# Graph attention and FFN on one core: all five engine lists reordered, PSUM banks assigned anew

## The chip, the core and the metric

The kernel runs on one core of a Trainium2 chip. The core has TensorE (PE, matrix products), VectorE (DVE), ScalarE (ACT), GpSimd (POOL) and SyncE (SP), which here only issues DMAs. Each engine works through a list of its own, in order, and the lists meet only in semaphores. The metric is the device time of one execution in microseconds (us), less is better.

## The reference

Two layers over 64 graphs of 256 nodes with 256 features and 8 heads of 32.

```
layer 0:  q, k = x@Wq + bq, x@Wk + bk;  attn = softmax(q k^T / sqrt(32))
          out  = sum over r of (attn * (adj == r)) @ (x@Wv[r] + bv[r])
          x1   = LN(x + out@Wo + bo);   x2 = LN(x1 + gelu(x1@W1 + b1)@W2 + b2)
layer 1:  q, k, v = x2@Wq, x2@Wk, x2@Wv;   e = leaky(q k^T)
          attn = softmax(where(adj > 0, e, -9e15));   h = LN(attn @ v)
          y    = LN(concat(h, x2) @ Wffn^T) + x2
```

adj holds only 0 and 1 in this data; a general path behind a flag serves other values and does not run.

## The kernel before

A graph passes through four stages, and one turn of the loop works on four graphs at once, one in each stage: `body(g0, g1, g2, g3)`. `turns` (L93) runs turns with some stages missing at both ends, and a hardware loop of full turns between them; 61 of the 67 turns are full. Each engine has its own `body`, a list written out by hand, with a wait in front of each step that needs one. The engines' numbering is offset by one: PE's g2 is the graph that ACT, DVE and POOL call g1 in the same stretch of time. A turn therefore makes one graph of work for every engine, and PE's list of a turn is the same set of products each time.

The steps that the text below speaks of, with their helpers:

- PE, attention of layer 0: `projection("wq")` and `("wk")` and `vee` (values) from the split x; `score_rows(p)` (L1029) for the row maxima; `score_cols(p)` (L1037) for the transposed scores; `both(g)` (weighted values and denominators); `one(g)` (values under the mask adj == 1); `out_projection`.
- PE, FFN: `transposed(B_X1T, x1)`, `up(0..3)`, `down(0..3)`, then `transposed(B_X2T, x2)`.
- PE, layer 1: `projection("lq")`, `("lk")`, `row_products` (lv), `masked_rows(p)` (L960), `turn(p)` (eight transposes of exponentiated scores), `row_values`, `transposed(B_HN, att)` (called the HN transposes below), `transposed(B_N1T, n1)` (the n1 transposes), `half_ffn` twice.
- ACT: `exp_cols(p)` (L529) after each `score_cols`; `exp_rows(p)` (L508); copies out of PSUM (L498); `low(p)` (L502); gelu.
- DVE: `statistics` / `centre` (L680) / `rescale` (L686) are the three pieces of a layer norm, LN_H being that of h in layer 1; `per_head` (L744) in front of it; the split remainders `lo_part` (L659); the comparisons `rel1` (L776) and `off_q` (L811) on the adjacency; `known` (L803), which checks that the adjacency is 0 or 1, and the small minimum `lowest` (L848) behind it.
- POOL: `masked(p)` (L408), two multiplications each, four a graph: the attention weights times rel1, begun when `exp_cols(0)` is done; the remainders `low` (L402); `make_rstd` (L396, L398) for each layer norm.
- SP: `stack(h, dst)` (L309), three DMAs inside SBUF that lay q and k of two heads out for the scores: `stack_a` for layer 0, `stack_r` for layer 1; both read the buffer qk. `load` (L314) brings x, xT, adj and adjT of a graph.

PSUM has eight banks of one 128x512 tile each; `bank(b)` is one, `pair[s]` two neighbours. The table B_... (L200) says which step uses which bank, and a PE step waits until the last reader of its bank is done.

Of the kernel before, what the change touches and what calls it, by code (L numbers as in the profile page):

```python
# [26 lines left out]
H = 8  # L27
# [4 lines left out]
KT = D // P  # L32
# [11 lines left out]
NEG = -9e15  # L44
# [63 lines left out]
def build(nc, x, xT, adj, adjT, w):  # L108
    ctx = ExitStack()
    with ctx:  # L110
# [172 lines left out]
        def _(sp):  # L283
# [42 lines left out]
            def body(g0, g1, g2, g3):  # L326
                if g1 is not None:
                    load(adj_q, adj, g1, "(t p) n -> p t n", ld_adj_r)
                if g2 is not None:
                    stack(0, stack_a, stacked_a)  # L330
                if g3 is not None:
                    load(xt, xT, g3, "(t p) n -> p t n", ld_xt)
                if g2 is not None:
                    stack(2, stack_a, stacked_a)
                    stack(3, stack_a, stacked_a)
                    sp.wait_ge(ashift.sem, ashift.at(g2))
                    for s in range(2):
                        sp.dma_start(stack_a[STK + s:STK + s + 1, 0, :, :].bitcast(F32),
                                     shift_a[32 * s:32 * s + H, :].bitcast(F32)).then_inc(ashifted.sem, 16)
                    if path.general:  # L340
                        load_x_terms(g2)
                if g1 is not None:
# [3 lines left out]
                    stack(2, stack_r, stacked_r)  # L346
                if g3 is not None:
                    if ran(g3, 1):
                        sp.wait_ge(known_done.sem, known_done.at(g3 - 1))
                    load(adj_a, adjT, g3, "(t p) n -> p t n", ld_adj_a)  # L350
                if g1 is not None:
                    stack(3, stack_r, stacked_r)
# [3 lines left out]
                if g3 is not None:  # L356
                    if ran(g3, 1):
                        sp.wait_ge(res_a_done.sem, res_a_done.at(g3 - 1))
                    load(xn, x, g3, "(t p) c -> p t c", ld_xn)
                    sp.wait_ge(qk_split.sem, qk_split.at(g3))  # L360
                    stack(1, stack_a, stacked_a)
# [19 lines left out]
        def _(pool):  # L381
# [48 lines left out]
            def body(g0, g1, g2, g3):  # L430
                if g1 is not None:
                    pool.wait_ge(ln_mv[LN_A].sem, ln_mv[LN_A].at(g1))
# [8 lines left out]
                    low(act_lo[:, 0], act[:, 0], act_hi[:, 0]).then_inc(act_split.sem, 1)  # L441
                if g0 is not None:
# [22 lines left out]
                if g3 is not None:  # L465
                    pool.wait_ge(xt_hi_done.sem, xt_hi_done.at(g3))
                    low(xt_lo[:], xt[:], xt_hi[:]).then_inc(xt_split.sem, 1)
                if g2 is not None:
                    pool.wait_ge(att_hi_done.sem, att_hi_done.at(g2))
                    low(att_lo[:], att[:], att_hi[:]).then_inc(att_split.sem, 1)  # L470
# [20 lines left out]
        def _(act_e):  # L491
# [39 lines left out]
            def body(g0, g1, g2, g3):  # L531
                if g0 is not None:
                    copy(v_r[:], bank(B_LV)).then_inc(rv_done.sem, 1)
                    act_e.wait_ge(sr_mm.sem, sr_mm.at(g0, 2))
                    low(1, B_RR[1]).then_inc(low_done.sem, 1)
                    act_e.wait_ge(sr_mm.sem, sr_mm.at(g0, 3))
                    low(2, B_RR[2]).then_inc(low_done.sem, 1)
                if g2 is not None:
                    act_e.wait_ge(q_mm.sem, q_mm.at(g2, 1))
                    if ran(g2, 2):  # L540
                        act_e.wait_ge(stacked_r[3].sem, stacked_r[3].at(g2 - 2))
                    biased(0, B_Q, bq_c).then_inc(qk_hi_done.sem, 1)
                if g0 is not None:
                    act_e.wait_ge(low_r_done.sem, low_r_done.at(g0, 1))
                    exp_rows(0).then_inc(exp_r_done.sem, 1)
                if g2 is not None:
                    act_e.wait_ge(v_mm.sem, v_mm.at(g2, 1))
                    copy(v_a[:, 0], bank(B_V[0])).then_inc(v_done.sem, 1)
                    act_e.wait_ge(v_mm.sem, v_mm.at(g2))
                    copy(v_a[:, 1], bank(B_V[1])).then_inc(v_done.sem, 1)  # L550
                    act_e.wait_ge(q_mm.sem, q_mm.at(g2))
                    biased(1, B_K, bk_c).then_inc(qk_hi_done.sem, 1)
                if g1 is not None:
                    act_e.wait_ge(x1t_mm.sem, x1t_mm.at(g1))
                    copy(x1t_hi[:], bank(B_X1T)).then_inc(x1t_hi_done.sem, 1)
                if g0 is not None:
                    act_e.wait_ge(turned_mm.sem, turned_mm.at(g0, 1))
                    copy(probs[:, :, 0], pair[B_TN[0]][:]).then_inc(probs_r.sem, 1)
                    act_e.wait_ge(sr_mm.sem, sr_mm.at(g0))
                    low(3, B_RR[3]).then_inc(low_done.sem, 1)  # L560
                if g1 is not None:
# [5 lines left out]
                    gelu(2, B_UP[2]).then_inc(act_done.sem, 1)  # L567
                    act_e.wait_ge(act_split.sem, act_split.at(g1, 1))
                    act_e.wait_ge(up_mm.sem, up_mm.at(g1))
                    gelu(3, B_UP[3]).then_inc(act_done.sem, 1)  # L570
                if g0 is not None:
                    act_e.wait_ge(low_r_done.sem, low_r_done.at(g0, 2))
                    exp_rows(1).then_inc(exp_r_done.sem, 1)
# [4 lines left out]
                    act_e.wait_ge(turned_mm.sem, turned_mm.at(g0, 2))  # L578
                    copy(probs[:, :, 1], pair[B_TN[1]][:]).then_inc(probs_r.sem, 1)
# [27 lines left out]
                if g1 is not None:  # L607
                    act_e.wait_ge(sr_mm.sem, sr_mm.at(g1, 1))
                    low(0, B_RR[0]).then_inc(low_done.sem, 1)

# [16 lines left out]
        def _(dve):  # L627
# [121 lines left out]
            def body(g0, g1, g2, g3):  # L749
                if g2 is not None:  # L750
                    dve.wait_ge(qk_hi_done.sem, qk_hi_done.at(g2))
                    biased_low(1, B_K, bk_c).then_inc(qk_split.sem, 1)
                if g1 is not None:
                    dve.wait_ge(x1t_hi_done.sem, x1t_hi_done.at(g1))
                    lo_part(x1t_lo, B_X1T, x1t_hi).then_inc(x1t_split.sem, 1)
                if g0 is not None:
                    dve.wait_ge(low_done.sem, low_done.at(g0, 3))
                    leaky(2, B_RR[2]).then_inc(leaky_done.sem, 1)
                    dve.wait_ge(leaky_done.sem, leaky_done.at(g0, 2))
                    lowest_row(1).then_inc(low_r_done.sem, 1)  # L760
# [521 lines left out]
```

## Time and profile before

| | us |
|---|---|
| median of 3 runs | 3328.57 |
| lowest and highest | 3326.73, 3330.99 |
| profiled execution, its time | 3329.45 |
| profiled execution, its span | 3327.6 |
| PE busy / DVE busy / ACT busy / POOL busy | 3141.7 / 2795.0 / 2098.1 / 1474.6 |
| mean granted TensorE clock | 0.991 of full |

The profile page gives busy times per engine, the span in 40 slices, the DMA queues, the chain that ended last and the costliest groups of instructions. The trace behind it answers by engine, line, tile and stretch. A PE row of two matmuls such as `1526.04 0.40 ... x2` starts the next such row 0.235 us later: matmuls overlap, and their ends are modelled.

### The profile page before, as it was taken

How to read it: one execution, taken by the hardware profiler on the slowest of the kernel's cores; microseconds unless marked ns; L12 is line 12 of the kernel's file. 1: busy time of each engine (PE TensorE's matmuls, PEld its weight loads, DVE VectorE, ACT ScalarE, POOL GpSimd, SP SyncE). 2: the span in 40 equal slices, each digit the busy share in tenths (PEclk: the TensorE clock that was granted, in tenths of full speed). 3: DMA queues.
4: the chain of work that ended last, by engine and by line, in shares of the span. 5: the costliest groups of instructions: out<-in, count | busy, mean ns of one | idle time of the engine just before them, and what ended most of it. 6: DMA issues, size and time to landing. Idle time of an engine off the chain costs nothing.

```text
span 3327.6 us, 77390 instructions
## 1 busy us (share of the span) xinstructions
PE 3141.7 (94%) x28930; PEld 2713.8 (82%) x28930; DVE 2795.0 (84%) x4892; ACT 2098.1 (63%) x4300; POOL 1474.6 (44%) x1549
## 2 busy tenths in 40 slices
PE   3899999999999999999999999999999999999996
PEld 2788888888888888888888888888888888888885
DVE  3688888888888888888888888888888888888885
ACT  2466666666666666666666666666666666666664
POOL 1345345344444444444444444444444444444441
PEclk8999999999999999999999999999999999999998
DMA  3333333333433433423433433433433433433331
GB/s 105 81 89 82 101 81 86 102 79 85 105 76 86 107 76 86 107 76 86 107 76 86 107 76 86 107 76 86 107 76 86 107 76 86 106 77 86 104 74 33
DMA packets 217643, 292.63 MB, mean 88 GB/s; under 512 B 31492, under 2 KB 119048, under 8 KB 217608
## 3 DMA queue, kind: packets, MB, share of 16 engines
q1 hardware_dynamic: 217608, 292.16, 34.2%
q8 instruction: 22, 0.36, 0.0%
q14 instruction: 13, 0.11, 0.0%
HBM read 72.89 MB, written 16.78 MB: 27 GB/s over the span
## 4 chain that ended last, share of the span: by engine, by line
PE 62%; SPq 10%; DVE 7%; POOL 7%; DMA 6%; ACT 4%; issue 4%; POOLq 0%; DVEq 0%; ACTq 0%
PE pair L920 32%; PE pair L950 11%; SPq L309 8%; DMA stack_a<-qk 5%; PE pair L974 5%; POOL probs L408 4%; PE pair L1033 3%; PE pair L965 3%; DVE n L686 3%; PE pair L966 3%; ACT probs L529 2%; POOL rstd L398 2%; PE pair L925 2%; DVE qk L738 2%; ACT qk L516 2%
## 5 line engine op out<-in xcount | busy, mean ns | idle before, releaser
L402 POOL TENSOR_TENSOR act_r_lo<-act,act_r_hi 128x512 fp32r<-128x512 f32 x256 | 345.7, 1356 | 654.0 <-DVE act_r_hi L765 523.0
L502 ACT ACTIVATE leaky_s<-pair 128x1024 f32<-128x1024 f32 x256 | 260.5, 1029 | 436.6 <-PE pair L966 436.6
L508 ACT ACTIVATE leaky_s<-leaky_s,low_r 128x256 f32<-128x256 f32 x1024 | 506.6, 496 | 10.9 <-DVE low_r L728 4.1
L732 DVE TENSOR_REDUCE mx_a<-pair 128x4 f32<-128x1024 f32 x256 | 306.4, 1217 | 114.0 <-PE pair L1033 113.9
L408 POOL TENSOR_TENSOR probs<-probs,rel 128x512 f32<-128x512 f32 x256 | 309.6, 1229 | 164.2 <-ACT probs L529 164.2
L396 POOL TENSOR_TENSOR rstd<-mv,eps 128x2 f32<-128x2 f32 x256 | 72.6, 284 | 660.0 <-DVE mv L675 660.0
L529 ACT ACTIVATE probs<-pair 128x1024 f32<-128x1024 f32 x256 | 263.1, 1029 | 127.8 <-PE pair L1042 125.4
L498 ACT ACTIVATE probs<-pair 128x1024 f32<-128x1024 f32 x256 | 260.5, 1019 | 86.2 <-PE pair L974 81.9
L724 DVE TENSOR_TENSOR leaky_s<-pair,leaky_s 128x1024 f32<-128x1024 f32 x256 | 306.7, 1219 | 5.2 <-ACT leaky_s L502 5.2
L728 DVE TENSOR_REDUCE low_r<-leaky_s 128x4 f32<-128x1024 f32 x256 | 304.0, 1208 | 0.0
L408 POOL TENSOR_TENSOR leaky_s<-probs,rel 128x512 f32<-128x512 f32 x256 | 300.7, 1204 | 0.0
L974 PE MATMUL pair<-ident,leaky_s 128*128 128x128 f32 x2048 | 267.8, 274 | 10.0 <-ACT leaky_s L508 9.8
L965 PE MATMUL pair<-stack_r 96*128 96x256 f32 x1024 | 271.6, 360 | 4.9 <-DMA stack_r<-qk 2.3
L966 PE MATMUL pair<-off_q,identb 128*128 128x256 bf16 x1024 | 259.4, 285 | 0.0
L523 ACT ACTIVATE act<-pair,bias_col 128x256 f32<-128x256 f32 x512 | 209.7, 473 | 73.6 <-PE pair L920 72.8
L974 PEld LDWEIGHTS pair<-ident,leaky_s 128*128 128x128 f32 x2048 | 231.3, 141 | 13.1 <-ACT leaky_s L508 11.1
L920 PE MATMUL pair<-xt_r_hi,w_hi 128*128 128x256 f32 x1024 | 209.5, 286 | 29.0 <-DVE xt_r_lo L659 29.0
L965 PEld LDWEIGHTS pair<-stack_r 96*128 96x128 f32 x1024 | 205.1, 200 | 32.0 <-issue 28.8
L853 DVE RECIPROCAL att<-pair 128x512 f32<-128x512 f32 x64 | 214.9, 3358 | 14.6 <-PE pair L950 12.6
L398 POOL TENSOR_TENSOR rstd<-rstd,power 128x2 f32<-128x2 f32 x256 | 216.3, 845 | 20.1
L950 PE MATMUL pair<-probs,v_a 128*32 128x256 f32 x3072 | 205.7, 386 | 13.3 <-ACT probs L529 13.3
L402 POOL TENSOR_TENSOR att_r_lo<-att,att_r_hi 128x512 fp32r<-128x512 f32 x64 | 82.6, 1290 | 305.2 <-DVE att_r_hi L864 305.2
(180 smaller groups left out, 9112.3 us busy)
## 6 DMA issues: line engine op xcount, KB each, us to landing
stack_a<-qk SPq DMA_DIRECT2D x768, 128.0 KB, 2.9
stack_r<-qk SPq DMA_DIRECT2D x768, 128.0 KB, 2.4
xt<-in_xT SPq DMA_DIRECT2D x64, 256.0 KB, 3.2
adj_a<-in_adjT SPq DMA_DIRECT2D x64, 256.0 KB, 3.1
xn<-in_x SPq DMA_DIRECT2D x64, 256.0 KB, 3.0
adj_q<-in_adj SPq DMA_DIRECT2D x64, 256.0 KB, 3.0
out<-n SPq DMA_DIRECT2D x64, 256.0 KB, 2.2
probs<-in_w SPq DMA_DIRECT2D x4, 512.0 KB, 5.1
```

The source lines that it names most:

```text
L402: return nc.gpsimd.tensor_tensor(dst, src, hi, ALU.subtract)
L408: last = nc.gpsimd.tensor_tensor(masked_p[g][:, h], probs[:, g, h], rel1[:], ALU.mult)
L508: last = nc.scalar.activation(leaky_s[:, p % SLOTS, k, t], leaky_s[:, p % SLOTS, k, t], ACT.Exp, bias=low_r[:, p, k, t:t + 1], accum_out=d ...
L529: return nc.scalar.activation(probs[:, g, 2 * q:2 * q + 2], pair[b][:], ACT.Exp, scale=SCALE)
L724: return nc.vector.tensor_tensor(leaky_s[:, p % SLOTS], pair[b][:], leaky_s[:, p % SLOTS], ALU.max)
L728: return nc.vector.tensor_reduce(low_r[:, p], leaky_s[:, p % SLOTS], AX.X, ALU.max, negate=True)
L732: return nc.vector.tensor_reduce(mx_a[:, :, p * NG:(p + 1) * NG].rearrange("p t h -> p h t"), pair[b][:], AX.X, ALU.max)
L920: last = mm(dst, lhs(i, t), rhs(j, t), start=start and n == 0, stop=stop and n == len(steps) - 1, skip_group_check=skip)
L950: last = mm(bank(b)[h * DH:(h + 1) * DH, g, :], v(t, g * GH + h), pr(h, t), start=first and t == 0, stop=stop and t == NT - 1, skip_group_ ...
L965: mm(dst, stack_r[:, 0, slot(h), t * P:(t + 1) * P], stack_r[:, 1, slot(h), :], start=True, stop=False)
L966: last = mm(dst, identb[:], off_q[:, t, :], start=False, stop=True)
L974: last = nc.tensor.transpose(pair[b][:, k, c, t * P:(t + 1) * P], leaky_s[:, p % SLOTS, k, t, c * P:(c + 1) * P], ident[:])
```

## The change

No instruction is added or removed on any engine; every list is put in another order and the banks are given out anew. What the text below speaks of:

- PE: `score_cols(1)` comes directly after `score_cols(0)`, and the HN transposes after both; `masked_rows(1)` and `(2)` of a graph move to the next turn, around the q projection; `turn(0)` moves ahead of the k projection, `turn(1)` ahead of the up products; `down(3)` moves behind `turn(3)`; `one(0)` moves from ahead of the second half of the FFN to behind `masked_rows(0)`.
- DVE: in the stretch of LN_H, `off_q` comes in ahead of `centre`, and `known` in the place of the x cast between `centre` and `rescale`; the cast and the reciprocal of the row sums move ahead to `shift`; `rel1` moves behind the statistics of the FFN's norm; `lowest` leaves the place ahead of the long reciprocal.
- POOL: the remainder of the next x ahead of the masks instead of behind them; that of the attention output at the head of the next turn.
- SP: all four `stack_a` copies in one row behind the split of k; in the kernel before, copy 1, a load, copy 0, a load, copies 2 and 3.
- ACT: `exp_rows(1)` before the first turned copy, the turned copy 1 between gelu 2 and gelu 3, the bias on k last.

```diff
-        B_AO, B_ADEN, B_Q, B_K, B_WO, B_X1T, B_RV, B_HN = 2, 4, 3, 7, 4, 6, 3, 4
-        B_DN, B_N1T, B_FFN, B_AMT, B_X2T, B_LQ, B_LK, B_LV = 3, 3, 0, 7, 5, 3, 6, 1
+        B_AO, B_ADEN, B_Q, B_K, B_WO, B_X1T, B_RV, B_HN = 2, 6, 7, 6, 1, 4, 4, 2
+        B_DN, B_N1T, B_FFN, B_AMT, B_X2T, B_LQ, B_LK, B_LV = 1, 1, 3, 4, 1, 4, 7, 7
         B_X = 0
-        B_V, B_UP = (5, 4), (7, 1, 3, 2)
-        B_RR, B_TN, B_AR, B_AC = (2, 3, 0, 2), (1, 0, 2, 1), (0, 3, 2, 3), (3, 1, 3, 3)
+        B_V, B_UP = (5, 7), (4, 6, 1, 5)
+        B_RR, B_TN, B_AR, B_AC = (0, 2, 1, 0), (0, 1, 1, 3), (3, 1, 2, 3), (2, 3, 2, 0)
...
# SP, behind the stack_r copies
+                if g3 is not None:
+                    sp.wait_ge(qk_split.sem, qk_split.at(g3))
+                    stack(0, stack_a, stacked_a)
+                    stack(1, stack_a, stacked_a)
+                    stack(2, stack_a, stacked_a)
+                    stack(3, stack_a, stacked_a)
                     load(adj_a, adjT, g3, "(t p) n -> p t n", ld_adj_a)
...
# POOL, behind the four act remainders, ahead of the masks
+                if g3 is not None:
+                    pool.wait_ge(xt_hi_done.sem, xt_hi_done.at(g3))
+                    low(xt_lo[:], xt[:], xt_hi[:]).then_inc(xt_split.sem, 1)
...
# DVE, the stretch of LN_H
                     lo_part(x2t_lo, B_X2T, x2t_hi).then_inc(x2t_split.sem, 1)
+                    dve.wait_ge(ld_adj_r.sem, ld_adj_r.at(g1))
+                    nc.vector.tensor_scalar(off_q[:], adj_q[:], 0, NEG, ALU.is_le, ALU.mult).then_inc(off_done.sem, 1)
                 if g0 is not None:
                     dve.wait_ge(ln_mv[LN_H].sem, ln_mv[LN_H].at(g0))
                     centre(LN_H, n1, LG1, n1)
-                if g3 is not None:
-                    dve.wait_ge(ld_xt.sem, ld_xt.at(g3))
-                    nc.vector.tensor_copy(xt_hi[:], xt[:]).then_inc(xt_hi_done.sem, 1)
+                if g2 is not None and not path.general:
+                    dve.wait_ge(rel1_done.sem, rel1_done.at(g2))
+                    nc.vector.scalar_tensor_tensor(adj_a[:], adj_a[:], 0, rel1[:], ALU.is_equal, ALU.add,
+                                                   accum_out=known[:]).then_inc(known_done.sem, 1)
                 if g0 is not None:
                     dve.wait_ge(ln_mid[LN_H].sem, ln_mid[LN_H].at(g0))
                     dve.wait_ge(ln_rstd[LN_H].sem, ln_rstd[LN_H].at(g0))
...
# DVE, end of the turn: x1's remainder, then k's, in this order
+                    dve.wait_ge(x1t_hi_done.sem, x1t_hi_done.at(g2))
+                    lo_part(x1t_lo, B_X1T, x1t_hi).then_inc(x1t_split.sem, 1)
+                if g3 is not None:
+                    dve.wait_ge(qk_hi_done.sem, qk_hi_done.at(g3))
+                    biased_low(1, B_K, bk_c).then_inc(qk_split.sem, 1)
...
# PE, after the row values
                     pe.wait_ge(ashifted.sem, ashifted.at(g3))
+                    if ran(g3, 2):
+                        pe.wait_ge(att_r_done.sem, att_r_done.at(g3 - 2))
                     score_cols(0, B_AC[0]).then_inc(sta_mm.sem, 1)
+                    score_cols(1, B_AC[1]).then_inc(sta_mm.sem, 1)
                 if g1 is not None:
                     pe.wait_ge(att_r_done.sem, att_r_done.at(g1))
                     transposed(B_HN, att).then_inc(hn_mm.sem, 1)
-                if g3 is not None:
-                    score_cols(1, B_AC[1]).then_inc(sta_mm.sem, 1)
...
# PE, the n1 transposes: no longer behind the q split of layer 1
                 if g1 is not None:
-                    if ran(g1, -1):
-                        pe.wait_ge(rqk_split.sem, rqk_split.at(g1 + 1, 1))
+                    if ran(g1, -2):
+                        pe.wait_ge(probs_a.sem, probs_a.at(g1 + 2))
                     pe.wait_ge(ln_done[LN_H].sem, ln_done[LN_H].at(g1))
                     transposed(B_N1T, n1).then_inc(n1t_mm.sem, 1)
...
# PE, ahead of the up products
+                    pe.wait_ge(leaky_done.sem, leaky_done.at(g1, 3))
+                    turn(1, B_TN[1]).then_inc(turned_mm.sem, 1)
                 if g2 is not None:
                     pe.wait_ge(x1t_split.sem, x1t_split.at(g2))
                     up(0, B_UP[0]).then_inc(up_mm.sem, 1)
```

## Rows read from the trace of the kernel before

**Rows 1.** Page, part 5: group, count | busy us, mean ns | idle before, releaser.

```profile
L974 PE MATMUL pair<-ident,leaky_s 128*128 128x128 f32 x2048 | 267.8, 274 | 10.0 <-ACT leaky_s L508 9.8
```

**Rows 2.** Busy time by stretch: PE, PEld, DVE, ACT, POOL, then clock, DMA share, GB/s.

```profile
600.00:3100.00 2500.00, 2432.02 (x22574) 2103.95 (x22574) 2168.84 (x3796) 1627.74 (x3346) 1151.45 (x1200) 1.00 0.35 89
```

**Rows 3.** Waits of PE, 600 to 3100 us: total us, times, longest.

```profile
PE pair L1033 <- DMA stack_a<-qk: 21.8, 68, 0.7
PE pair L920 <- DVE xt_r_lo L659: 21.3, 49, 0.4
PE pair L938 <- DVE qk L840: 10.7, 50, 0.2
PE pair L950 <- ACT probs L529: 9.8, 50, 0.2
```

**Rows 4.** PE's timeline, one turn: start, us, line, operation, [idle before].

```profile
1520.56 0.74 PE L1042 MATMUL pair<-stack_a 98*128 98x256 f32 x4
1521.35 0.66 PE L938 MATMUL pair<-ident,att 128*128 128x128 f32 x4
...
1523.60 1.07 PE L950 MATMUL pair<-probs,v_a 128*32 128x256 f32 x16 [0.20 <-ACT probs L529]
...
1526.04 0.40 PE L920 MATMUL pair<-x2t_hi,lq_hi 128*128 128x256 f32 x2
...
1529.25 0.65 PE L938 MATMUL pair<-ident,n 128*128 128x128 f32 x4 [0.22 <-DVE qk L840]
...
1548.10 0.60 PE L938 MATMUL pair<-ident,x 128*128 128x128 f32 x4
...
1550.11 0.50 PE L920 MATMUL pair<-xt_r_hi,w_hi 128*128 128x256 f32 x2 [0.44 <-DVE xt_r_lo L659]
...
1556.15 1.21 PE L1033 MATMUL pair<-stack_a 96*128 96x256 f32 x8 [0.33 <-DMA stack_a<-qk]
...
1559.11 0.73 PE L1033 MATMUL pair<-stack_a 96*128 96x256 f32 x4 [0.37 <-DMA stack_a<-qk]
```

**Rows 5.** DVE's timeline, the same turn, the stretch of LN_H.

```profile
1522.16 0.69 DVE L744 TENSOR_TENSOR n<-pair,rden_r 128x512 f32<-128x512 f32 x1 [0.72 <-PE pair L938]
...
1524.07 0.69 DVE L659 TENSOR_TENSOR x2t_lo<-pair,x2t_hi 128x512 fp32r<-128x512 f32 x1
1524.67 0.88 DVE L680 SCALAR_TENSOR_TENSOR n<-n,mv,norm 128x256 f32<-128x256 f32 x2
1525.47 0.42 DVE L833 CAST xt_r_hi<-xt 128x512 fp32r<-128x512 f32 x1
1526.03 1.17 DVE L686 SCALAR_TENSOR_TENSOR n<-n,rstd,norm 128x256 f32<-128x256 f32 x1
1527.13 1.39 DVE L686 SCALAR_TENSOR_TENSOR n<-n,rstd,norm 128x256 f32<-128x256 f32 x1
```

**Rows 6.** POOL's timeline beside it: the mask multiplications.

```profile
1522.44 2.29 POOL L408 TENSOR_TENSOR probs<-probs,rel 128x512 f32<-128x512 f32 x2 [2.15 <-ACT probs L529]
...
1525.67 1.25 POOL L408 TENSOR_TENSOR probs<-probs,rel 128x512 f32<-128x512 f32 x1
1526.88 1.36 POOL L408 TENSOR_TENSOR probs<-probs,rel 128x512 f32<-128x512 f32 x1
```

**Rows 7.** DVE's timeline: known and lowest, and x1's remainder.

```profile
1518.46 0.66 DVE L803 SCALAR_TENSOR_TENSOR adj_a<-adj_a,rel 128x512 int32<-128x512 int32 x1
...
1531.18 0.62 DVE L848 TENSOR_TENSOR lowest<-lowest,known 128x1 f32<-128x1 f32 x1
...
1549.37 0.69 DVE L659 TENSOR_TENSOR xt_r_lo<-pair,xt_r_hi 128x512 fp32r<-128x512 f32 x1 [0.19 <-ACT xt_r_hi L498]
```

**Rows 8.** SP's timeline: six stack_a issues in a row.

```profile
1504.76 3.80 SPq L309 DMA_DIRECT2D stack_a<-qk  x6
```

**Rows 9.** The profile page, part 6: issues, KB, us from issue to landing.

```profile
stack_a<-qk SPq DMA_DIRECT2D x768, 128.0 KB, 2.9
stack_r<-qk SPq DMA_DIRECT2D x768, 128.0 KB, 2.4
```

More of the change, by code:

```diff
@@ L326, in body @@
             def body(g0, g1, g2, g3):
-                if g1 is not None:
-                    load(adj_q, adj, g1, "(t p) n -> p t n", ld_adj_r)
                 if g2 is not None:
-                    stack(0, stack_a, stacked_a)
+                    load(xn, x, g2, "(t p) c -> p t c", ld_xn)
                 if g3 is not None:
@@ L555, in body @@
                     copy(x1t_hi[:], bank(B_X1T)).then_inc(x1t_hi_done.sem, 1)
+                if g2 is not None:
+                    act_e.wait_ge(v_mm.sem, v_mm.at(g2))
+                    copy(v_a[:, 1], bank(B_V[1])).then_inc(v_done.sem, 1)
                 if g0 is not None:
-                    act_e.wait_ge(turned_mm.sem, turned_mm.at(g0, 1))
-                    copy(probs[:, :, 0], pair[B_TN[0]][:]).then_inc(probs_r.sem, 1)
                     act_e.wait_ge(sr_mm.sem, sr_mm.at(g0))
@@ L567, in body @@
                     gelu(2, B_UP[2]).then_inc(act_done.sem, 1)
+                if g0 is not None:
+                    act_e.wait_ge(turned_mm.sem, turned_mm.at(g0, 2))
+                    copy(probs[:, :, 1], pair[B_TN[1]][:]).then_inc(probs_r.sem, 1)
+                if g1 is not None:
                     act_e.wait_ge(act_split.sem, act_split.at(g1, 1))
@@ L795, in body @@
                     nc.vector.tensor_tensor(res[:], bank(B_DN), x1[:], ALU.add).then_inc(res_m_done.sem, 1)
-                if g2 is not None:
-                    dve.wait_ge(amt_mm.sem, amt_mm.at(g2))
-                    shift(bank(B_AMT)[0:H, 0, :], shift_a, g2, ashift_hi, ashift)
-                if g1 is not None:
                     dve.wait_ge(res_m_done.sem, res_m_done.at(g1))
                     statistics(LN_M, res, g1)
-                if g2 is not None and not path.general:
-                    nc.vector.scalar_tensor_tensor(adj_a[:], adj_a[:], 0, rel1[:], ALU.is_equal, ALU.add,
-                                                   accum_out=known[:]).then_inc(known_done.sem, 1)
+                if g2 is not None:
+                    dve.wait_ge(ld_adj_a.sem, ld_adj_a.at(g2))
+                    nc.vector.tensor_scalar(rel1[:], adj_a[:], 1, None, ALU.is_equal).then_inc(rel1_done.sem, 1)
                 if g1 is not None:
@@ L845, in body @@
                     lo_part(n1t_lo, B_N1T, n1t_hi).then_inc(n1t_split.sem, 1)
-                if g2 is not None and not path.general:
-                    dve.wait_ge(known_done.sem, known_done.at(g2))
-                    nc.vector.tensor_tensor(lowest[:], lowest[:], known[:], ALU.min).then_inc(lowest_done.sem, 1)
                 if g2 is not None:
@@ L858, in body @@
                     centre(LN_O, bank(B_FFN), LG2, result)
+                if g1 is not None:
+                    dve.wait_ge(low_done.sem, low_done.at(g1, 1))
+                    leaky(0, B_RR[0]).then_inc(leaky_done.sem, 1)
                 if g2 is not None:
@@ L1144, in body @@
                     down(1)
+                if g3 is not None:
+                    pe.wait_ge(mx_a_done.sem, mx_a_done.at(g3, 1))
+                    pe.wait_ge(stacked_a[3].sem, stacked_a[3].at(g3))
+                    score_rows(3, B_AR[3]).then_inc(sa_mm.sem, 1)
+                if g2 is not None:
                     pe.wait_ge(act_split.sem, act_split.at(g2, 3))
```

248 lines of the change are left out of this document (115 added, 133 removed).

## Prediction

> **What bounds the kernel now.** The page comes first: PE is busy 94% of the span, DVE 84%. Then the busy time by stretch: from 600 to 3100 us PE is busy 2432.0 of 2500 us at full clock [rows 2]. In PE's timeline the same step comes round every 50.0 us, one turn, so PE is the bound, short of some waits. The waits of PE name four, 63.6 us in 50 turns, 1.27 us a turn [rows 3]. That understates them. A matmul's modelled end lies 0.16 us past the start of its successor (0.40 long, 0.235 apart), so a wait costs its idle bracket plus 0.16. By the timeline [rows 4] a turn loses: ahead of up(0), for x1's remainder, 0.44+0.16 = 0.60; ahead of score_rows(0), for the stack_a copies, 0.49; ahead of score_rows(2), again for them, 0.53; ahead of both(0), for exp_cols, 0.36; ahead of the n1 transposes, for the q remainder of layer 1 that holds their bank, 0.38; and ahead of the HN transposes 0.22 without a bracket (score_cols(0) at 1520.56 takes 0.57 where nothing waits, the transposes start 0.79 later). Sum 2.58 us of 50.0: about 47.4 us are products, and the change leaves these alone. Only the waits can move, from -2.6 us a turn to any loss.
>
> **Part by part.** Letters: S is the start of score_cols(0), P that of x1's transposes.
>
> *The wait ahead of up(0), 0.60.* x1's transposes start at P, the remainder on DVE at P+1.27 (1548.10, 1549.37) and ends at P+1.96 [rows 4, 7]. New, turn(1) stands between masked_rows(3) and up(0). A turn is 267.8/256 = 1.05 us busy, less the overlap 0.89 [rows 1]. PE arrives at up(0) 0.89 later than the P+1.4 of before, at P+2.3, after the remainder. Gain 0.60. Turn(1) itself waits for leaky(2), which DVE does while PE is at vee(1) and the transposes; I take nothing for it, at most 0.3.
>
> *The stack_a copies, 0.49 and 0.53.* New, DVE makes the remainder of k behind that of x1: P+1.27, then 0.60 on (the distance of such rows at 1524.07 and 1524.67 [rows 5]) and two instructions of 0.88 together: P+2.75. SP then issues twelve copies without a load between, 3.80/6 = 0.63 apart [rows 8]. Those of score_rows(2) are complete with the ninth: P+2.8+8x0.63 = P+7.8, plus 2.4 us to landing as for stack_r, which also goes out in one row, or 2.9 as for stack_a now [rows 9]: P+10.2 to P+10.8. PE wants them at: 1559.11-1548.10 = 11.0, less the three waits of before, 1.62, plus turn(1), 0.89, so P+10.3. Wait 0 to 0.5; I take 0.3, the middle, as the copies are like stack_r's but more of them compete. Score_rows(0) needs the third copy, P+4.1+2.9 = P+7.0, and is wanted at about P+7.7: no wait. Gain 0.49+0.23 = 0.72.
>
> *HN transposes and exp_cols.* With score_cols(1) pulled ahead, the transposes start at S+1.13 after the copy of the row values is done: gain 0.22. The wait for exp_cols(1) ahead of both(0) stays, 0.36. From S to the lq projection it was 1526.04-1520.56 = 5.48; without the 0.22 it is 5.26 [rows 4]. And HN is now 0.34 later after S than before (0.79).
>
> *The norm LN_H, where I expect the loss.* Before: DVE's per_head starts 0.81 after HN, x2t_lo 1.91 after that, centre (two instructions), the x cast, and rescale, whose instructions take 1.17 and 1.39 us where such an instruction alone takes under 0.5 (centre, 0.88 for two) [rows 4, 5]. Beside them POOL multiplies the masks: 1525.67 to 1526.92, then a row starting 1526.88 that lasts 1.36 instead of 1.15 [rows 6]. The first rescale ends 0.28 after the first multiplication, the second 0.28 after the next (1528.24): the two engines take turns, one DVE instruction per multiplication, 1.31 us a pair. The little lowest, one element a partition, takes 0.62 there [rows 7]. So each DVE instruction of this kind that is caught behind the masks costs about 1.3 us.
>
> New list: per_head at S+1.13+0.81 = S+1.94, x2t_lo at S+3.85, off_q at S+4.45, centre at S+4.79 and S+5.19, known at S+5.6, rescale. POOL's third multiplication (the first that matters) keeps its distance: 1525.67-1522.44 = 3.23 behind the first, which starts 1.88 behind S: S+5.11 [rows 4, 6]. It comes between the two centre instructions. Known, which comes ahead of rescale in place of a cast, is then caught, and rescale twice, against two catches before. If the second centre instruction gets in first: multiplication to S+6.65, known (0.66 alone, 0.5 of it held [rows 7]) to S+7.2, multiplication to S+8.3, rescale to S+8.55, multiplication to S+9.7, rescale to S+9.95. If it is caught too, one more pair: S+10.8. PE comes to the n1 transposes at S+5.26+2.84 = S+8.10 (2.84: from 1526.04 to 1529.25 less 0.38). Wait 1.9 or 2.8 us against 0.38. The two starts lie 0.08 us apart, nearer than I can tell, so I take 2.4: loss 2.0. Neither known nor centre is seen beside a mask in this trace. The bounds: no new catch at all, then LN_H is done by S+8.95 at the latest with both rescales caught (wait 0.9, loss 0.5), or by S+7.2 with none (no wait, gain 0.4); at the other end both caught and off_q too, loss 3.4.
>
> The Trainium skill, "SBUF — State Buffer", section "Who interferes with whom", has a rule for this: a VectorE instruction with two SBUF inputs, or in a two-port mode, and a GpSimd instruction that reads SBUF hold the shared port pair exclusively, each for its whole length. By that rule known (adj_a and rel1) and centre (n and norm) are caught like rescale, and the loss is the 2.0; by the rows alone, were only rescale caught, it would be 0.5, and the sum a gain. This case's 1.17 and 1.39 us against 0.48 agree with the rule for rescale only.
>
> *Behind it.* The q and k remainders of layer 1 stand behind rescale on DVE, the twelve stack_r copies on SP behind them, masked_rows(0) on PE. All shift with the n1 transposes: the third copy lands 1.3+1.3+2.4 = 5.0 after rescale, PE arrives there 5.1 after (n1 transposes 0.4; both(1) 1.87, from 1523.60 to 1526.04 less 0.57; the FFN half and lv 1.42 each, like lq). No further wait, at most 0.2. The later output projection meets the attention remainder, which POOL now makes first: att_split follows one(1) by some 3 us and four steps lie between; nothing taken.
>
> *Edits at nothing.* The x cast and remainder ahead of the masks: POOL is busy 46% [rows 2] and idle there. rel1 and the reciprocals: DVE has 6.6 us free a turn. The turned copy between two gelus lies on ACT, a third free. If the covers go, each costs its own 0.4 to 1.3 us once a turn; PE would show it as a wait at the x2 transposes. Fill and drain, 3329.45-64x50.0 = 129 us in all, are reordered too; I take 0, within 5 either way.
>
> **Sum.** A turn: -0.60 - 0.72 - 0.22 + 2.0 = +0.46 us. 61 full turns: +28 us on the profiled execution's 3329.45, which lies 0.9 above the median: 3357 for the median.
>
> **Rivals.**
> 1. *Known and centre slip in ahead of the masks, or aren't held by them* (faster). For it: 0.08 us decide the order, and nobody has seen known held here. Against it: lowest, a still smaller instruction, is. The wait at n1 is then 0 to 0.9, loss at most 0.5: -1.54+0.5 = -1.0 a turn, -63 us: 3266; with no wait at all 3211. It decides if LN_H is done before S+8.10+0.38+1.54 = S+10.0, where gains and loss cancel; the less, the faster.
> 2. *Both centre and known caught, and stack copies at 2.9 us* (clearly slower). -0.60-0.22-0.49+2.4+0.2 = +1.3 a turn: 3408. For it: the waiting engine took its turn at 1526.88. Against: the cheaper landing of a run of copies.
> 3. *It cancels.* Centre in first and copies landing at 2.4: -0.60-1.02-0.22+1.55 = -0.3; with small waits at turn(1) and masked_rows(0) 0.0: within 7 us of 3328.6. PE stays the bound and the change only moves waits.
>
> **Chances.** Forecast 42%, rival 1 26%, rival 2 18%, rival 3 14%. 0.2% is 6.7 us, about what a measurement of this kernel can tell from no change. Faster by more 0.26, within 0.14, slower 0.60. The range 3262 to 3405 reaches to the middle of rival 1 and the edge of rival 2; the forecast's own is 3338 to 3390.
>
> **What would show it.** The waits of PE: no row for xt_r_lo ahead of up, one for the n1 transposes (PE L938 on DVE n L686) of some 2 us a turn. On DVE, known at 1.2 us or more instead of 0.66, and a rescale of n still at 1.2 to 1.4. Stack_a: one wait a turn, under 0.6. The prediction is wrong if PE waits under 1 us for n, or if known keeps 0.66: then look for rival 1; and if PE shows a wait at turn(1), masked_rows(0) or out_projection that I set at nothing.

## The result, and the profile after

The changed kernel took 3254.16 us (median of 4 runs, 3245.96 to 3258.36) against 3328.11 us for the kernel before (3326.73 to 3330.99), a ratio of 0.977 with a 95% interval of 0.975 to 0.979. The forecast was slower, 3357 us, range 3262 to 3405. It was wrong in sign, and the time lies below the range; of the cases named, rival 1 came closest (3266 with small losses, 3211 with none).

The page and the window and wait views of after, with the columns of the rows of before [rows 1 to 3, 9]:

```profile
PE 3119.1 (96%) x28930; PEld 2711.1 (83%) x28930; DVE 2710.2 (83%) x4892; ACT 2063.7 (63%) x4300; POOL 1473.1 (45%) x1549
L976 PE MATMUL pair<-ident,leaky_s 128*128 128x128 f32 x2048 | 269.6, 275 | 6.7 <-ACT leaky_s L502 5.8
...
stack_a<-qk SPq DMA_DIRECT2D x768, 128.0 KB, 2.4
stack_r<-qk SPq DMA_DIRECT2D x768, 128.0 KB, 2.4
```

```profile
600.00:3100.00 2500.00, 2469.69 (x23132) 2153.17 (x23130) 2147.82 (x3891) 1638.33 (x3422) 1177.29 (x1230) 1.00 0.39 91
```

```profile
PE pair L940 <- DVE n L686: 21.1, 51, 0.5
PE pair L952 <- ACT probs L523: 9.1, 51, 0.2
```

PE is busy 2469.7 of 2500 us, where it was 2432.0 [rows 2], at the full clock in both. The remainder of x1 and the stack_a copies are gone from its waits [rows 3]. The 10.7 us for the q remainder have become 21.1 us for n, that is for the end of LN_H, in 51 turns: 0.41 us each, where about 2.2 was forecast (2.4 with the 0.16 by which a bracket understates a wait). A copy of stack_a now lands in 2.4 us instead of 2.9 [rows 9]. A turn, measured from one start of score_cols(0) (S) to the next and averaged from 600 to 3000 us, fell from 50.08 to 48.88 us. 61 turns times 1.20 are 73 us, and the medians differ by 74: nothing of note happened in fill and drain.

PE's timeline of after, one turn (start, us, line, operation, [idle before]); it answers to [rows 4]:

```profile
1513.51 1.04 PE L976 MATMUL pair<-ident,leaky_s 128*128 128x128 f32 x8
1514.30 0.48 PE L922 MATMUL pair<-xt_r_hi,w_hi 128*128 128x256 f32 x2
...
1521.91 1.36 PE L1035 MATMUL pair<-stack_a 96*128 96x256 f32 x8
...
1533.49 1.12 PE L1044 MATMUL pair<-stack_a 98*128 98x256 f32 x8
1534.45 0.60 PE L940 MATMUL pair<-ident,att 128*128 128x128 f32 x4
...
1536.16 1.07 PE L952 MATMUL pair<-probs,v_a 128*32 128x256 f32 x16 [0.18 <-ACT probs L523]
...
1538.60 0.40 PE L922 MATMUL pair<-x2t_hi,lq_hi 128*128 128x256 f32 x2
...
1542.01 0.66 PE L940 MATMUL pair<-ident,n 128*128 128x128 f32 x4 [0.41 <-DVE n L686]
```

The up products at 1514.30 and the two score_rows of stack_a at 1521.91 start without a wait. The heads' transposes start at S + 0.96, lq at S + 5.11 (before: 5.48), and n1's transposes at S + 8.52 (before: 8.69).

DVE and POOL of after in the stretch of LN_H, S = 1533.49; they answer to [rows 5, 6]:

```profile
1535.20 0.69 DVE L744 TENSOR_TENSOR n<-pair,rden_r 128x512 f32<-128x512 f32 x1 [0.84 <-PE pair L940]
...
1536.94 0.66 DVE L659 TENSOR_TENSOR x2t_lo<-pair,x2t_hi 128x512 fp32r<-128x512 f32 x1
1537.52 0.41 DVE L805 TENSOR_SCALAR off_q<-adj_q 128x512 bf16<-128x512 int32 x1
1537.85 0.87 DVE L680 SCALAR_TENSOR_TENSOR n<-n,mv,norm 128x256 f32<-128x256 f32 x2
1538.64 0.68 DVE L811 SCALAR_TENSOR_TENSOR adj_a<-adj_a,rel 128x512 int32<-128x512 int32 x1
...
1539.25 2.70 DVE L686 SCALAR_TENSOR_TENSOR n<-n,rstd,norm 128x256 f32<-128x256 f32 x2
```

```profile
1537.60 0.39 POOL L390 TENSOR_TENSOR rstd<-mv,eps 128x2 f32<-128x2 f32 x1
1538.06 0.81 POOL L392 TENSOR_TENSOR rstd<-rstd,power 128x2 f32<-128x2 f32 x1
1538.84 2.83 POOL L402 TENSOR_TENSOR probs<-probs,rel 128x512 f32<-128x512 f32 x2
```

Known (DVE L811) takes 0.68 us, against 0.66 in before, where POOL did not hold it [rows 7]. The third mask multiplication is the first of the two on the last line. It starts at 1538.84, 0.20 us behind known, instead of ahead of it. The two rescales take 2.70 us together, two catches as before.

### The profile page after: what moved, and what is told of

It reads as the page before. It is cut to its first block, busy times and chain, and to the rows that moved or that the text cites. A ratio compares the mean times of both kernels' runs of the same rounds, so it can differ in the third digit from the quotient of the medians.

```text
span 3252.1 us, 77634 instructions
## 1 busy us (share of the span) xinstructions
PE 3119.1 (96%) x28930; PEld 2711.1 (83%) x28930; DVE 2710.2 (83%) x4892; ACT 2063.7 (63%) x4300; POOL 1473.1 (45%) x1549
## 4 chain that ended last, share of the span: by engine, by line
PE 81%; DVE 14%; issue 2%; SPq 1%; DMA 1%; ACT 1%; POOL 0%; DVEq 0%; ACTq 0%; POOLq 0%
PE pair L922 44%; PE pair L952 11%; PE pair L976 7%; DVE n L686 5%; PE pair L1035 4%; PE pair L967 4%; PE pair L968 4%; PE pair L940 3%; PE pair L1044 2%; PE pair L927 2%; DVE n L680 2%; DVE n L744 1%; DVE x2t_lo L659 1%; DVE stats L671 1%; SPq L309 1%
## 5 line engine op out<-in xcount | busy, mean ns | idle before, releaser
L396 POOL TENSOR_TENSOR act_r_lo<-act,act_r_hi 128x512 fp32r<-128x512 f32 x256 | 334.8, 1315 | 748.7 <-DVE act_r_hi L886 550.3
L402 POOL TENSOR_TENSOR probs<-probs,rel 128x512 f32<-128x512 f32 x256 | 327.2, 1300 | 124.7 <-ACT probs L523 124.7
L492 ACT ACTIVATE v_r<-pair 128x512 f32<-128x512 f32 x64 | 38.2, 597 | 269.8 <-PE pair L922 269.8
L922 PE MATMUL pair<-w_hi,act_r_hi 128*128 128x256 f32 x1024 | 208.8, 286 | 0.0
```

The costliest lines, as they stand in the source:

```text
L396: return nc.gpsimd.tensor_tensor(dst, src, hi, ALU.subtract)
L402: last = nc.gpsimd.tensor_tensor(masked_p[g][:, h], probs[:, g, h], rel1[:], ALU.mult)
L492: return nc.scalar.activation(dst, src, ACT.Copy)
L922: last = mm(dst, lhs(i, t), rhs(j, t), start=start and n == 0, stop=stop and n == len(steps) - 1, skip_group_check=skip)
```

## The experiments

Turns are means from 600 to 3000 us; S is the start of score_cols(0), and the starts of n1's transposes are medians over the same turns. Each run's interval for the ratio to before, 95%, stands in the table; before was run anew beside each group of runs, with medians of 3327.84 to 3330.45 us. A delay is given as the shift of off_q's start; the expectations call the three 0.36, about 0.56 and 0.72 us.

| kernel | us | ratio to before | turn, us | n1's transposes |
|---|---|---|---|---|
| before | 3328.11 | 1 | 50.08 | S+8.68 |
| after | 3254.16 | 0.975 to 0.979 | 48.88 | S+8.52 |
| a1: delay 0.33 | 3273.21 | 0.981 to 0.985 | 49.17 | S+8.84 |
| a10: delay 0.53 | 3441.82 | 1.032 to 1.035 | 51.88 | S+10.89 |
| a2: delay 0.66 | 3495.98 | 1.049 to 1.053 | 52.56 | S+11.02 |
| a3: known late | 3231.92 | 0.969 to 0.972 | 48.55 | S+8.17 |
| a9: off_q early | 3278.48 | 0.983 to 0.986 | 49.23 | S+8.83 |
| a8: both | 3237.69 | 0.971 to 0.973 | 48.56 | S+8.23 |
| a11: a8, masked_rows together | 3254.71 | 0.976 to 0.979 | 48.88 | S+8.24 |
| a4: HN between the scores | 3252.61 | 0.976 to 0.979 | 48.85 | S+8.51 |
| a5: turn(1) back | 3282.25 | 0.984 to 0.988 | 49.45 | not moved |
| a6: loads between the copies | 3405.25 | 1.021 to 1.025 | 51.19 | not moved |
| b1: before, known in LN_H | 3441.76 | 1.032 to 1.036 | 51.96 | S+10.25 |
| b2: before, copies in a row | 3270.98 | 0.981 to 0.984 | 49.13 | S+8.68 |

### Is the forecast's mechanism real? Delays of LN_H (a1, a10, a2)

Into DVE's list of the kernel after, ahead of off_q, one or two statistics of n1 that nobody uses (a10: the second one over 128 columns of a constant). In this and the later cuts, waits, guards and loops around the lines are left out:

```
                 lo_part(x2t_lo, B_X2T, x2t_hi).then_inc(x2t_split.sem, 1)
+                nc.vector.bn_stats(spare[:, 0], n1[:, 0])           # a1, a10, a2
+                nc.vector.bn_stats(spare[:, 1], n1[:, 1])           # a2
+                nc.vector.bn_stats(spare[:, 1], norm[:, 0, 0:128])  # a10
                 nc.vector.tensor_scalar(off_q[:], adj_q[:], 0, NEG, ALU.is_le, ALU.mult)
```

> The changed kernel with one more statistics instruction (0.36 us, one SBUF input, its result unused) on VectorE between x2t_lo and off_q. Theory of turns: known is issued 0.2 us ahead of the third mask multiplication in the changed kernel; with 0.36 more it comes behind it, is caught, and each later pair of instructions takes turns: LN_H ends about 1.2 us later, the wait of PE ahead of the n1 transposes grows from 0.57 to about 1.8 a turn, known lasts over 1.0 us, and the time is 3254 + 61x1.2 = 3327. Rival, queue length alone: LN_H ends 0.36 later, the time is 3254 + 22 = 3276, known stays at 0.68.

> As the one before with two such instructions, 0.72 us. Theory of turns: the second centre instruction is caught too, LN_H ends about 2.4 us later than in the changed kernel: 3254 + 61x2.4 = 3400. Rival, queue length alone: 3254 + 61x0.72 = 3298.

> The kernel after with 0.36 + about 0.2 us of statistics into an unused buffer between x2's low part and off_q, half-way between the two delays already run (0.36 us: 3273; 0.72 us: 3496). Theory (a cliff: as soon as the third mask product starts ahead of the second centring or of known, VectorE's instruction waits for its end): known or centring is stretched by about 1 us, n1's transposes start 1.3 us or more later than in the kernel after, and the total is at least 3254 + 61 x 1.5 = 3345 us, more where PE's clock falls. Rival (queue length alone, 61 x 0.57): 3289 us.

One delay cost 19 us, what its length asks for (n1's transposes 0.32 us later), so the expectation of a caught known missed. A further 0.2 us cost 169 us more. Between the two lies the step that the forecast had assumed. DVE and POOL of a10, S = 1463.4:

```profile
1467.93 0.41 DVE L811 TENSOR_SCALAR off_q<-adj_q 128x512 bf16<-128x512 int32 x1
1468.26 1.79 DVE L681 SCALAR_TENSOR_TENSOR n<-n,mv,norm 128x256 f32<-128x256 f32 x2
1469.97 1.66 DVE L817 SCALAR_TENSOR_TENSOR adj_a<-adj_a,rel 128x512 int32<-128x512 int32 x1
...
1471.56 2.65 DVE L687 SCALAR_TENSOR_TENSOR n<-n,rstd,norm 128x256 f32<-128x256 f32 x2
```

```profile
1467.76 0.69 POOL L393 TENSOR_TENSOR rstd<-rstd,power 128x2 f32<-128x2 f32 x1
1468.41 2.67 POOL L403 TENSOR_TENSOR probs<-probs,rel 128x512 f32<-128x512 f32 x2
```

The mask multiplication starts at 1468.41, while the first centre instruction runs, and has its turn before the second. So the second centre instruction takes 1.40 us (medians over the turns; 1.79 for the two here against 0.87 in after), known 1.66 instead of 0.68, and n1's transposes start at S + 10.89. In a1 the mask multiplication also starts ahead of known, by 0.19 us, and yet known keeps 0.69: the row that begins first is here not the one that goes first. DVE and POOL of a1:

```profile
1507.56 0.88 DVE L681 SCALAR_TENSOR_TENSOR n<-n,mv,norm 128x256 f32<-128x256 f32 x2
1508.35 0.69 DVE L816 SCALAR_TENSOR_TENSOR adj_a<-adj_a,rel 128x512 int32<-128x512 int32 x1
```

```profile
1507.25 0.94 POOL L393 TENSOR_TENSOR rstd<-rstd,power 128x2 f32<-128x2 f32 x1
1508.16 3.21 POOL L403 TENSOR_TENSOR probs<-probs,rel 128x512 f32<-128x512 f32 x2
```

There POOL is the one that is held. The first of its two multiplications lasts 1.91 us (median) instead of 1.17, about to the end of known and one undisturbed length on. A reading that fits, but is not shown: once DVE had what both need, its next instruction followed without a gap that POOL could use. In a10, with DVE's starts 0.2 us later, POOL got in. What exactly decides who has the next turn is not settled by these runs. That 0.2 us decide it is shown.

### Known alone (a3 and b1)

In after known is moved behind the low part of n1's transposes (a3). In before it is moved the other way, between the x cast and the rescales (b1):

```
a3:              centre(LN_H, n1, LG1, n1)
-                nc.vector.scalar_tensor_tensor(adj_a[:], adj_a[:], 0, rel1[:], ...accum_out=known[:])
                 rescale(LN_H, n1, row(LB1))
                 ...
                 lo_part(n1t_lo, B_N1T, n1t_hi).then_inc(n1t_split.sem, 1)
+                nc.vector.scalar_tensor_tensor(adj_a[:], adj_a[:], 0, rel1[:], ...accum_out=known[:])
b1:              nc.vector.tensor_copy(xt_hi[:], xt[:])
+                nc.vector.scalar_tensor_tensor(adj_a[:], adj_a[:], 0, rel1[:], ...accum_out=known[:])
```

> The changed kernel with known moved out of the norm LN_H, behind n1t_lo. Theory: rescale follows centre at once, LN_H ends 0.6 us or more earlier and PE's wait ahead of the n1 transposes (0.57 a turn) goes: 3254 - 61x0.57 = 3219. Rival: known, now caught beside the masks (1.2 us), pushes the long reciprocal and what hangs on it, and PE waits ahead of out_projection instead: within 7 us of 3254.

> The kernel before with known moved into LN_H, between the x cast and rescale, as the change has it, and nothing else. Theory of turns: the cast starts 0.2 us ahead of the third mask multiplication there, so known comes behind it and is caught: known lasts 1.1 us or more, LN_H ends 1.3 to 1.6 us later, the n1 transposes wait that much more: 3328 + 61x1.3 = 3407. Rival, queue length alone: known's own 0.74 at most, 3328 + 45 = 3373, or nothing if the gap ahead of rescale hides it.

a3 is the fastest kernel of the study: 3231.92 us, 22 us below after. Its only wait of PE from 600 to 3100 us with a bracket is this one:

```profile
PE pair L952 <- ACT probs L523: 9.3, 52, 0.2
```

The expectation of 3219 had the whole wait of 0.57 us go. Only 0.35 went (S + 8.52 to S + 8.17). The rescales now start at S + 5.49, 0.10 us behind the end of POOL's power (the reciprocal root of LN_H, S + 5.39), and LN_H ends at S + 8.12; PE still waits for it, too briefly for a bracket.

b1 shows the forecast's number where the order is the forecast's: DVE and POOL of b1.

```profile
1525.84 1.66 DVE L832 SCALAR_TENSOR_TENSOR adj_a<-adj_a,rel 128x512 int32<-128x512 int32 x1
...
1527.43 2.68 DVE L686 SCALAR_TENSOR_TENSOR n<-n,rstd,norm 128x256 f32<-128x256 f32 x2
```

```profile
1525.70 2.83 POOL L408 TENSOR_TENSOR probs<-probs,rel 128x512 f32<-128x512 f32 x2
```

The multiplication starts 0.14 us ahead of known, known takes 1.66 us, both rescales are caught behind it, and n1's transposes start 1.57 us later than in before. So "a DVE instruction with two operands in SBUF, caught behind the masks, costs a turn" holds for known (1.66) and for centre (1.40 in a10), not for rescale alone. This is the exclusive lock that the Trainium skill gives in "SBUF — State Buffer", section "Who interferes with whom", and the traces agree in both directions: 1.66 us for known here, 1.91 us for the multiplication in a1.

### What else stands ahead of the rescales (a4, a9, a8)

```
a4 (PE):         score_cols(0, B_AC[0]).then_inc(sta_mm.sem, 1)
+                transposed(B_HN, att).then_inc(hn_mm.sem, 1)
                 score_cols(1, B_AC[1]).then_inc(sta_mm.sem, 1)
-                transposed(B_HN, att).then_inc(hn_mm.sem, 1)
a9 (DVE):        rescale(LN_M, x2, row(E2))
+                nc.vector.tensor_scalar(off_q[:], adj_q[:], 0, NEG, ALU.is_le, ALU.mult)
                 ...
                 lo_part(x2t_lo, B_X2T, x2t_hi).then_inc(x2t_split.sem, 1)
-                nc.vector.tensor_scalar(off_q[:], adj_q[:], 0, NEG, ALU.is_le, ALU.mult)
a8: the edits of a3 and a9 together
```

> The changed kernel with the HN transposes back between score_cols(0) and score_cols(1), on PE alone. Theory: per_head and all of LN_H on VectorE come 0.45 us earlier, the wait at the n1 transposes goes, exp_cols(1) is not later since ScalarE is still at exp_cols(0): 3254 - 61x0.5 = 3224. Rival: exp_cols(1) comes later by the 0.4 us and both(0) waits that much more: 3254 within 10 us.

> The kernel after with off_q alone moved ahead of per_head; known stays between centring and rescaling. Theory (a long VectorE instruction is stretched if it starts while GpSimd holds what they share, and off_q's 0.42 us are the only gain): known starts 0.4 us earlier, ahead of the third mask product, and is not stretched; the two rescalings are stretched as in the kernel after; n1's transposes start at S + 8.3 and the total is 3240 to 3254 us. Rival (the queue's length alone counts, and the earlier rescalings fall outside the third mask product too): 3219 us.

> The kernel after with two VectorE instructions taken out of the stretch between the transposed heads and the norm's rescale: the sum over the mask products (known, 0.68 us) moved behind the low part of n1's transposes, and the adjacency mask off_q moved ahead of per_head. Theory (the norm's end sets the start of n1's transposes, and both instructions lie in its way): the kernel with known alone moved took 3232 us and the wait ahead of n1's transposes still held about 0.2 to 0.4 us a turn through off_q and the centring; off_q gone moves centring 0.4 us earlier, n1's transposes start at S + 7.8, and the total is 3232 - 61 x 0.38 = 3209 us. Rival (ScalarE's and GpSimd's reciprocal root, which ends at S + 5.1, holds the rescaling, so that an earlier centring gains nothing): 3225 to 3232 us. Rival (off_q ahead of per_head delays per_head itself): 3240 us.

None gained on the kernel it started from (after for a4 and a9, a3 for a8). In a4 per_head starts 0.48 us earlier, but off_q then falls beside the second mask multiplication, lasts 0.68 instead of 0.41, and centre starts at S + 4.36 as in after. The time is the rival's, the reason is not: both(0) starts where it did in after, at S + 2.68 against 2.67. In a9 centre and known are 0.33 us earlier, and the cost is 24 us. DVE and POOL of a9:

```profile
1498.81 0.87 DVE L680 SCALAR_TENSOR_TENSOR n<-n,mv,norm 128x256 f32<-128x256 f32 x2
1499.60 0.69 DVE L811 SCALAR_TENSOR_TENSOR adj_a<-adj_a,rel 128x512 int32<-128x512 int32 x1
...
1500.93 2.62 DVE L686 SCALAR_TENSOR_TENSOR n<-n,rstd,norm 128x256 f32<-128x256 f32 x2 [0.64 <-POOL rstd L392]
```

```profile
1499.42 1.41 POOL L392 TENSOR_TENSOR rstd<-rstd,power 128x2 f32<-128x2 f32 x1
```

Here the small power on POOL, two numbers a partition, is the one that waits: it lasts 1.41 us instead of 0.81 and ends 0.55 us behind known (S + 6.05 and S + 5.50, medians), and the rescales wait for it (0.64 us). Of the two expectations neither had this. In a8 known is away, and the power ends at S + 5.45, 0.55 us behind the second centre instruction; in a3 it ends at S + 5.39. So the rescales start at S + 5.55, and in a3 at S + 5.49, though centre is 0.33 us earlier in a8: the rival with the power as the limit had the right mechanism (3238, 6 us over the end of its 3225 to 3232). The third guess, 3240, is nearer as a number, but per_head is not delayed: it starts at S + 1.72 as in after. a8's turn equals a3's (48.56 and 48.55); the 6 us between their medians lie outside the stretch from 600 to 3000 us, and what makes them was not followed.

### The gains one by one (b2, a5, a6)

```
b2 (before, SP):   stack 0, stack 2, stack 3 in a row, then the loads of adj_q and xt
                   (were ahead of and behind stack 0; stack 1 is issued earlier in both)
a5 (after, PE):    turn(1) behind the up products instead of ahead of them
a6 (after, SP):    stack 0, load adj_q, stack 1, load adj_a, stack 2, stack 3 (was: adj_q, stacks 0 to 3, adj_a)
```

> The kernel before with the stack_a copies of a graph issued in one row, the two loads behind them. Theory: the waits ahead of score_rows(0) and (2), 0.37 and 0.35 a turn on average, go: 3328 - 61x0.7 = 3285. Rival: what counts is when the remainder of k is done, not the loads between: half of it or less stays, 3306 or more.

> The changed kernel with turn(1) behind the up products instead of ahead. Theory: PE waits 0.6 us a turn for x1's remainder ahead of up(0), as before the change: 3254 + 37 = 3291. Rival: the stack_a copies then have the slack that turn(1) gives, and a wait is only moved: under 3270.

> The changed kernel with the loads of adj_q and adj_a put between the stack_a copies (behind copy 0 and behind copy 1), as before the change. Theory: the issues of copy 2 end 1.1 us later and land 0.5 later: score_rows(2) waits 0.9 to 1.3 us: 3254 + 61x1.1 = 3321. Rival: landing has slack of 1 us here: under 3270.

b2 is 57 us faster than before with nothing else changed, 0.95 us a turn: PE's waits for stack_a are gone and the copy lands in 2.4 us. The two steps ahead of score products that waited are shorter by 0.35 and 0.37 us, the score products behind them by 0.10 and 0.09. a5 gives back 28 us, 0.57 a turn, and the wait for x1's remainder comes back as it was [rows 3]:

```profile
PE pair L922 <- DVE xt_r_lo L659: 21.7, 50, 0.4
```

a6 puts two loads between the copies: it costs 151 us, far over the 67 expected. The page gives 2.9 us for a landing again, and PE waited for stack_a 86.1 us in 52 places between 600 and 3000 us, 2.5 us at most. With the 0.16 that a bracket leaves out that is 2.0 us a turn, 123 us in 61 turns; the rest is the clock (last section). Why the wait is nearly twice the 1.1 us expected was not followed.

### One change of kind fewer on PE (a11)

```
-                masked_rows(1, B_RR[1]).then_inc(sr_mm.sem, 1)
                 ... (wq)
+                masked_rows(1, B_RR[1]).then_inc(sr_mm.sem, 1)
                 masked_rows(2, B_RR[2]).then_inc(sr_mm.sem, 1)
```

> The kernel with both instructions moved (a8_both_moved), and PE's masked_rows(1) put directly ahead of masked_rows(2), so that the order is wq, masked_rows(1), masked_rows(2) in place of masked_rows(1), wq, masked_rows(2). Theory (each change from one kind of product to another costs PE about 0.085 us, by the step lengths): one change fewer, 61 x 0.085 = 5 us below a8_both_moved. Rival (changes of kind cost nothing by themselves, only the order against other engines does): equal within 2 us, or above it where the later scores hold ScalarE or VectorE.

A miss: 17 us slower than a8. The two masked_rows together take 1.874 us instead of 1.903, so the boundary gave 0.03, not 0.085, and wq and wo beside it are 0.02 longer each. But the value projection ahead of the first turn takes 1.83 instead of 1.63 us, and the turn behind it 0.85 instead of 0.79: the second pair's scores come one projection later. That what waits for them is later too would explain it, but which engine holds PE there was not followed.

## Why the prediction was wrong, step by step

**The wait ahead of up(0): right.** Forecast gain 0.60; from the start of masked_rows(3) to that of the next step it was 1.657 us and is 1.058. a5 puts turn(1) back and loses 0.57. Turn(1) waits for nothing.

**The stack_a copies: mechanism right, the sum met by luck.** Forecast gain 0.72, of it 0.49 and 0.23. The waits that went are 0.37 and 0.35 on average (my one turn had shown 0.49 and 0.53), so the whole loss was 0.72, and all of it went: of the two landings the cheap one, 2.4 us, came true. By b2 the repair alone is worth 0.95 a turn, because the products behind a wait were longer too. I had kept 0.3 for a wait that doesn't exist, and taken 1.02 instead of 0.72 for the loss; the two errors cancel.

**HN transposes and exp_cols: right.** From S to lq went from 5.48 to 5.11, 0.37 where 0.22 was forecast. In a4, where the HN transposes follow score_cols(0) as in before, they start at S + 0.48 and not S + 0.79: that step takes 0.48 us and not 0.57, so the wait had been 0.31. The wait for exp_cols stays at 0.35.

**The norm LN_H: this step failed.** Forecast: loss 2.0 a turn, n1's transposes at S + 10.0 to 10.9. Measured: S + 8.52, a wait of 0.57 (0.41 bracket and 0.16) where 0.38 stood, a loss of 0.19. PE's arrival there, forecast for S + 8.10, is S + 7.95 (lq at S + 5.11, and 2.84 us for lq and lk without a wait); that part was near. What failed is the order of centre, known and the third mask multiplication. By the steps of the forecast, medians over the turns of after:

| start behind S | forecast | after |
|---|---|---|
| HN transposes | 1.13 | 0.96 |
| per_head | 1.94 | 1.72 |
| x2t_lo | 3.85 | 3.45 |
| off_q | 4.45 | 4.03 |
| centre, both | 4.79, 5.19 | 4.36, 4.76 |
| known | 5.6 | 5.15 |
| third mask multiplication | 5.11 | 5.36 |

Two errors add up to 0.7 us. DVE's list runs 0.4 us earlier than I had it: 0.17 from the start of HN, 0.05 in per_head, and 0.17 because I carried over 1.91 us from per_head to x2t_lo, where the statistics between them take 1.74 and the rest had been a wait. And the third multiplication is 0.25 later, since it does not keep its distance from the first: between them stands POOL's reciprocal root, whose first instruction lasts 0.39 instead of 0.20 beside off_q, which makes 0.18 of it. (In a1 a statistics instruction stands in off_q's place at the same start, and POOL's instruction lasts 0.19.) So known starts 0.2 us ahead of the multiplication and not 0.5 behind it. I had put the margin at 0.08 us "nearer than I can tell", and nevertheless split it only between one catch and two; that both instructions could slip in ahead needed a shift of no more than 0.5 us, and had 26%.

The mechanism itself stands. Delay the stretch by 0.53 us and the very sequence of the second branch appears: a10's transposes start at S + 10.89, where the forecast gave S + 10.8 for both caught, and it takes 3442 us. The order and the catches are as forecast; that the two ends lie so near is partly luck, since one more pair of 1.31 us on the forecast's S + 9.95 would be S + 11.3. Known beside a mask is 1.66 us in a10 and b1, as the sequence needs. It was the phase that was wrong, far more than the price.

**Behind it, and the edits at nothing: one term missing.** No wait came at turn(1), masked_rows(0) or the output projection. But the steps in which PE waits for nothing became longer by 0.30 in sum. The larger parts, which make 0.25 of it, are the down products 5.74 to 6.02 us, wo and wk 0.08 each, score_rows 0.05, less 0.07 in wf and 0.08 each in the turns and masked_rows. Part of it is seen at the starts: the first product of a step of another kind is 0.48 long and followed after 0.32 instead of 0.235 us. a11 shows that this is no fixed price of a boundary (0.03, not 0.085). Where the rest comes from stays open: no run takes the new bank table or ACT's new order alone.

**The sum.** -0.60 for x1, -0.72 for the copies, -0.37 from S to lq, +0.19 at n1, +0.30 in the products: -1.20 us a turn, as measured. Forecast +0.46; of the difference of 1.66 the norm makes 1.8, S to lq 0.15 and the products -0.30.

The conclusion "known keeps 0.66: then look for rival 1" was the right test. Rival 1's own number, 3266, was made with a loss of 0.5 at n1; with the 0.19 measured it would be 3246, 8 us too low, since the products' +0.30 outweighs the extra 0.15 from S to lq.

## What to carry to other kernels

A wait of one turn read from a timeline is a sample: take averages, and ask of each distance that is carried over whether a wait is in it. Where a forecast hangs on which of two instructions on different engines starts first and they lie within half a microsecond, it has two answers, not a middle: give both prices and an even chance, or make the margin large. The same holds for tuning: the fast order of this kernel lies 0.3 to 0.5 us from one that costs 190 us more, and moving the one DVE instruction out of the critical stretch (a3) gains 22 us. It also takes known out of the danger; centre stays in it, and no run delays a3. Put the copies that a product waits for in one row and the loads behind them: in the kernel before that alone gave 57 us (b2), where the whole change gave 74.

## What the runs showed of the hardware

**PE's clock fell after the long waits.** In before, after, a1 and a3 PE's granted clock is 1.00 from 600 to 3000 us. In a10 the turns come in two lengths, 51.3 us (27 of 45) and 52.8 us (18 of 45); the granted clock is 1.00 over each of the short ones and 0.97 over each of the long ones. Two turns of a10 by stretch (columns as in [rows 2]); the first line of each group is the wait for n, and the first group is a short turn, the second a long one:

```profile
1473.00:1474.30 1.30, 0.03 (x1) 0.04 (x1) 1.30 (x2) 0.00 (x0) 1.30 (x2) 1.00 0.00 0
1474.30:1475.30 1.00, 1.00 (x12) 0.67 (x16) 1.00 (x2) 0.34 (x1) 1.00 (x2) 1.00 0.00 0
1475.30:1476.30 1.00, 1.00 (x24) 0.65 (x20) 0.80 (x2) 0.26 (x1) 1.00 (x1) 1.00 0.00 0
...
1524.30:1525.60 1.30, 0.00 (x0) 0.00 (x0) 1.30 (x2) 0.00 (x0) 1.30 (x2) 1.00 0.00 0
1525.60:1526.60 1.00, 0.98 (x12) 0.70 (x16) 1.00 (x2) 0.29 (x1) 1.00 (x2) 1.00 0.00 0
...
1527.60:1528.60 1.00, 1.00 (x16) 0.35 (x8) 0.03 (x1) 0.00 (x0) 0.10 (x1) 0.50 0.49 100
1528.60:1529.60 1.00, 1.00 (x9) 0.63 (x4) 0.51 (x1) 0.00 (x0) 0.00 (x0) 0.50 0.87 195
```

Both turns waited 2.8 us for n. In the second the granted clock fell to 0.50, that is 1.2 instead of 2.4 GHz, 1.5 us after the end of the wait, for about 3.5 us, and PE lost 1.5 us there. In half of the long turns it fell like that, in the other half at about the end of the wait; why it didn't fall in the 27 short turns, whose wait is the same, these runs don't show. Over a10 that is 18/45 x 1.5 x 61 = 37 of the 188 us to after; n1's transposes, 2.37 us later, make 145. The same two lengths of turn stand in a2 (51.3 and 52.9, 36 of 45 long), b1 (51.5 and 53.3, 10 of 45) and a6 (50.7 and 52.1, 15 of 46), with 0.97 over the long ones, and there PE's wait is mostly 2.9, 1.8 and 1.8 us. a2's transposes are only 0.13 us later than a10's, 8 us in 61 turns; most of the 54 us between the two are its more frequent long turns. So in this kernel the waits of that size cost more than their length, which neither my forecast nor the expectations of a2, b1 and a6 had.

**Small instructions and those with one operand are held too.** POOL's power on 128x2 took 0.69 us in a10 and 1.41 us in a9, by what DVE ran beside it, and DVE's off_q, which has one operand, 0.68 instead of 0.41 in a4. In before the comparison rel1, also with one operand, takes 1.50 us in the 29 of 48 turns in which it starts while POOL is at a remainder of the activations, and 0.41 in the other 19, in which it starts between two such remainders. A short instruction on a side engine can thus be the late one.
